# A four-layer graph network on one core: the last weights turned by VectorE, a new order between attention and mean, and a split chain of denominators

## The reference

```
L0 binary:    relu(adj @ (max(sign(x),0) @ sign(w).T))
L1 attention: h = x @ W_sa; s = s_left[:,None] + s_right[None,:]
              e = where(adj != 0, exp(-leaky_relu(s, 0.01)), 0)
              x_a = (e / (sum(e,1) + 1e-5)) @ h;   x_b = adj @ (x @ W_gcnb) + b
              sigmoid(attn_a * x_a + attn_b * x_b),  attn_* = sigmoid([adj @ x, x] @ W* + b*)
L2 mean:      (A @ (x @ W + b)) / deg,  A = (adj != 0), deg = column sums of A
L3 two GAT layers: Wh, Ws = split(x @ W_stack[l]);  a = softmax(Wh @ Ws.T) * adj
              x = leaky_relu(a @ Wh + x, 0.01)
```

## Time and profile before

| | |
|---|---|
| time, median of 3 runs | 476.89 us (476.69 to 477.68) |
| the profiled execution | 477.23 us, of which the span from first to last instruction is 475.4 |
| TensorE busy | 463.0 us, 97% of the span, 1854 instructions |
| VectorE busy | 372.1 us, 78% |
| ScalarE busy | 232.3 us, 49% |
| GpSimd busy | 190.6 us, 40% |
| DMA | 20.68 MB, 8180 packets, 44 GB/s on the mean |
| chain of work that ended last | TensorE 87%, VectorE 7%, issue 2%, DMA 2% |

### The profile page before, as it was taken

One profiled execution on the slowest core, in us unless ns is written; L12 is line 12 of the kernel. 1 busy time (PEld: TensorE's weight loads), 2 busy tenths in 40 slices (PEclk: granted clock), 3 DMA queues, 4 the chain that ended last, 5 costly groups with the idle time before them and its releaser, 6 DMA issues.

```text
span 475.4 us, 5636 instructions
## 1 busy us (share of the span) xinstructions
PE 463.0 (97%) x1854; PEld 304.2 (64%) x1854; DVE 372.1 (78%) x832; ACT 232.3 (49%) x411; POOL 190.6 (40%) x186
## 2 busy tenths in 40 slices
PE   8999999999999999999999999899999999999993
PEld 6999745545555588877544444454557546778882
DVE  4688799999998599739236757998755698799984
ACT  5979529980889653323334532251332475342200
POOL 1444665631425058823001541361430064456641
PEclk9999999999999999999999999999999999999999
DMA  8856310000364100000000000000000000000001
GB/s 280 284 181 193 123 40 0 1 1 0 117 193 161 32 0 1 0 1 1 1 0 0 0 1 1 1 0 1 0 1 0 1 1 1 0 13 22 23 22 40
DMA packets 8180, 20.68 MB, mean 44 GB/s; under 512 B 1008, under 2 KB 4740, under 8 KB 8152
## 3 DMA queue, kind: packets, MB, share of 16 engines
q1 hardware_dynamic: 7144, 19.02, 12.3%
q0 software_dynamic: 464, 0.79, 0.7%
q10 hardware_dynamic: 544, 0.52, 0.3%
HBM read 18.94 MB, written 1.39 MB: 43 GB/s over the span
## 4 chain that ended last, share of the span: by engine, by line
PE 87%; DVE 7%; issue 2%; DMA 2%; SPq 1%; ACT 1%; POOLq 0%; POOL 0%; DVEq 0%
PE psum L1544 19%; PE psum L1359 11%; PE psum L1335 11%; PE psum L1581 9%; PE psum L1644 8%; PE psum L1316 6%; PE psum L1422 6%; PE psum L1524 4%; PE psum L1237 2%; PE psum L1497 2%; PE psum L1379 2%; PE psum L1615 2%; PE psum L1406 2%; DMA adj_rows<-in_adj_dram 2%; PE psum L1476 1%
## 5 line engine op out<-in xcount | busy, mean ns | idle before, releaser
L1544 PE MATMUL psum<-QT,xT 128*128 128x512 f32 (+3 forms) x264 | 108.3, 542 | 1.7 <-ACT ST L634 1.7
L440 POOL TENSOR_TENSOR es<-es,ST 128x512 f32<-128x512 f32 (+3 forms) x60 | 74.9, 1248 | 53.8 <-ACT ST L639 52.1
L634 ACT ACTIVATE ST<-psum 128x512 f32<-128x512 f32 (+3 forms) x66 | 36.1, 546 | 89.6 <-DVE rm L994 77.9
L1544 PEld LDWEIGHTS psum<-QT,xT 128*128 128x128 f32 (+1 forms) x264 | 48.1, 186 | 44.5 <-issue 38.2
L994 DVE TENSOR_TENSOR rm<-psum,rm 128x512 f32<-128x512 f32 (+3 forms) x60 | 37.4, 624 | 41.2 <-PE psum L1544 41.0
L376 POOL TENSOR_TENSOR rstd<-veps,nhalf 128x1 f32<-128x1 f32 (+1 forms) x44 | 29.4, 668 | 65.0 <-DVE veps L770 65.0
L1644 PE MATMUL psum<-Wh,ST 128*128 128x256 f32 (+3 forms) x242 | 55.1, 380 | 0.0
L1581 PE MATMUL psum<-ST,Wh 128*128 128x512 f32 (+3 forms) x132 | 53.9, 542 | 0.0
L404 POOL TENSOR_TENSOR esumb<-esumb,eb 128x1354 f32<-128x1354 f32 (+1 forms) x10 | 34.5, 3447 | 46.4 <-ACT eb L528 46.4
L1359 PE MATMUL psum<-eb,x_all 128*128 128x512 f32 (+3 forms) x132 | 51.8, 542 | 0.0
L1335 PE MATMUL psum<-adjT,x_all 128*128 128x512 f32 (+3 forms) x132 | 50.1, 542 | 0.0
(11 more groups left out here) (181 smaller groups left out, 781.7 us busy)
## 6 DMA issues: line engine op xcount, KB each, us to landing
adj_rows<-in_adj_dram SPq DMA_DIRECT2D x10, 677.0 KB, 5.2
rows<-in_adj_dram SPq DMA_DIRECT2D x10, 677.0 KB, 4.0
x_all<-in_x_dram SPq DMA_DIRECT2D x5, 256.0 KB, 4.5
out_dram<-xs SPq DMA_DIRECT2D x10, 128.0 KB, 1.7
W<-in_L_gnn_W_stack_dram SPq DMA_DIRECT2D x2, 512.0 KB, 6.4
adj_rows<-in_adj_dram SPq DMA_DIRECT2D x1, 338.5 KB
rows<-in_adj_dram SPq DMA_DIRECT2D x1, 338.5 KB
w0n<-in_L_gnn_weight_dram SPq DMA_DIRECT2D x1, 256.0 KB, 2.8
```

Source lines behind the costliest of these rows:

```text
L440: nc.gpsimd.tensor_tensor(es[0:r, g % 2, 0:w], es[0:r, g % 2, 0:w], buf(g)[0:r, j, 0:w], ALU.add)\
L1544: last = nc.tensor.matmul(psum[0:r, SB[n % 3], 0:w], xT[l][:, k, j * P:j * P + r], QT[:, k, c0:c1], start=(k == 0), stop=(k == KD - 1))
```

## The change

SyncE loads W3 a second time, as 32x32 blocks laid out so that VectorE's block transpose yields the whole transpose. Each layer comes by four DMAs with runs of 32 elements, into space that exp buffers leave free, ahead of the loads of adjacency rows 9 and 10. VectorE turns each layer in one instruction, and TensorE's 16 transposes and ScalarE's four copies go. Each layer has its own W3T buffer and its own PSUM bank.

TensorE's first group of sum transposes moves one place up, into the last but one row of exp products, the second to its end, the third and the first projection in among the last row's products. ScalarE counts row 0 before its exp tile 6. VectorE reads the sums earlier, finishes `coef` with three instructions over full tiles (`dent` is set to 1 at the start), and scales tiles 3 to 10 and makes the degrees' reciprocals after the first sums of attention. The masks move, too. GpSimd's bias sums run at least four tiles late.

In the turnover from chunk 0 to 1, the denominators' chain goes in three parts behind rounds 1, 3 and 5, and scale, add and leaky go behind rounds 6, 7 and 8. All other turnovers stay as they are.

```diff
+            def load_blocks(l):
+                sp.wait_ge(h_step.sem, RING + l + 1)
+                sp.wait_ge(den_added.sem, RING + l + 1)
+                for a in range(QUADS):
+                    sp.dma_start(W3B[l][a * BLOCK:(a + 1) * BLOCK, :, :].rearrange("u e (b v) -> u e b v", v=BLOCK),
+                                 w3[l].rearrange("(b u) (e a v) -> a u e b v", u=BLOCK, a=QUADS, v=BLOCK)[a]).then_inc(w3b_in[l].sem, 16)
+
             sp.wait_ge(agga_done.sem, T)
             for i in range(T):
+                if i >= T - 2:
+                    load_blocks(i - T + 2)
                 if i >= 2:
                     sp.wait_ge(deg_ready.sem, T + i - 1)
...
             rsqrt(NB, 0)
-            for i in range(T):
+            rsqrt(NB, 1)
+            low_half(0)
+            low_half(1)
+            rsqrt(NB, 2)
+            low_half(2)
+            rsqrt(NB, 3)
+            for i in range(3, T):
                 if i + 1 < T:
                     rsqrt(NB, i + 1)
                 low_half(i)
+                if i >= 4:
+                    add_bias2(i - 4)
+            for i in range(T - 4, T):
                 add_bias2(i)
...
-            i = 0
             exp_scores(RING - 1)
+            row_degree(0)
+            i = 1
             for j in range(RING, T):
                 exp_scores(j)
-                for _ in range(2 if i + T - j < T else 1):
+                for _ in range(2):
                     if i < T:
                         row_degree(i)
                         i += 1
-            while i < T:
-                row_degree(i)
-                i += 1
...
-            w3T_evac(0)
             gate(0)
             gate(1)
             m3_evac(0)
+            m3_evac(1)
             gate(2)
-            w3T_evac(1)
             high_half(0)
             scale_b2(0)
-            m3_evac(1)
...
+            def turn_w3(l):
+                dve.wait_ge(w3b_in[l].sem, 16 * QUADS)
+                if l == 1:
+                    dve.wait_ge(h_step.sem, RING + 3)
+                    dve.wait_ge(den_added.sem, RING + 3)
+                nc.vector.transpose(W3T[l][:, :, :, :].rearrange("p h e n -> p (h e n)"), W3B[l][:, :, :].rearrange("p e n -> p (e n)"))\
+                    .then_inc(w3T_ready.sem, 1)
...
+            turn_w3(0)
             den_sums(0)
+            turn_w3(1)
+            den_sums(1)
             dve.wait_ge(att_t_ready.sem, 1)
             own.link(nc.vector.tensor_scalar(att[:, :, :], att_t[:, :, :], 0.5, 0.5, ALU.mult, ALU.add))
+            scale_xb(0, 3)
             den_sums(2)
+            dve.wait_ge(den_read.sem, BANKS_T)
+            own.link(nc.vector.tensor_scalar(dent[:, :], dent[:, :], ATTN_EPS, None, ALU.add))
+            own.link(nc.vector.reciprocal(dent[:, :], dent[:, :]))
+            nc.vector.tensor_tensor(coef[:, :], dent[:, :], att[:, :, 0], ALU.mult).then_inc(coef_ready.sem, 1)
...
+            attn_sum(0)
+            scale_xb(3, 6)
+            attn_out(0)
+            attn_sum(1)
+            scale_xb(6, T)
+            norm_apply(NB, 0, vbuf[:, 0, :])
+            attn_sum(2)
+            attn_out(1)
             dve.wait_ge(deg_ready.sem, 2 * T)
...
-            attn_sum(0)
-            attn_sum(1)
-            attn_out(0)
-            attn_sum(2)
+            norm_apply(NB, 1, vbuf[:, 1, :])
+            attn_sum(3)
             mean_mask(3)
-            for i in range(T):
+            attn_out(2)
+            attn_sum(4)
+            norm_apply(NB, 2, vbuf[:, 2, :])
+            mean_mask(4)
+            attn_out(3)
+            attn_sum(5)
+            mean_mask(5)
+            for i in range(3, T):
                 if i + 1 < T:
                     attn_out(i + 1)
                 norm_apply(NB, i, vbuf[0:kk(i), i % 4, :])
                 if i + 3 < T:
                     attn_sum(i + 3)
-                if i + 4 < T:
-                    mean_mask(i + 4)
+                if i + 3 < T:
+                    mean_mask(i + 3)
...
                 soft_step(g + 1, 0)
                 soft_step(g + 1, 1)
-                den_blocks(g)
+                if g > 0:
+                    den_turn(g)
+                    den_gather(g)
+                    den_spread(g)
                 for s in range(last):
                     both(g + 1, s)
-                    if s == 0:
+                    if g == 0 and s == 1:
+                        den_turn(g)
+                    if g == 0 and s == 3:
+                        den_gather(g)
+                    if g == 0 and s == 5:
+                        den_spread(g)
+                    if s == add - 1:
                         scale_t(g)
...
-            turnover(0, T, 2)
+            turnover(0, T, 7)
...
+                        if j == T - 2 and (c, m) == (1, 1):
+                            turn_exps(0)
+                        if j == T - 1:
+                            last.then_inc(h_done.sem, 1)
+                            if (c, m) == (1, 0):
+                                turn_exps(2)
+                            if (c, m) == (1, 1):
+                                h_proj(0)
...
                 if j == T - 1:
-                    turn_exps(0)
+                    turn_exps(1)
                 h_part(j)
...
-            h_proj(0)
-            turn_w3(0)
             h_proj(1)
             h_proj(2)
             mul_w3(0)
-            turn_w3(1)
+            mul_w3(1)
             h_proj(3)
-            mul_w3(1)
```

More of the change, by code:

```diff
@@ L556, in _ @@
                     nc.scalar.activation(hT[:, m, c0:c1], bank(c * KD + m, 0, c1 - c0), ACT.Copy).then_inc(hT_ready.sem, 1)
[L558 to L565 removed]
             def m3_evac(l):
                 act.wait_ge(m3_ps.sem, l + 1)
[L569 removed]
+                nc.scalar.activation(M3[:, l, :, :], bank(2 + l).rearrange("p (k n) -> p k n", k=KD),
                                      ACT.Copy).then_inc(m3_ready.sem, 1)
@@ L907, in den_sums, with scale_xb @@
                 last.then_inc(den_read.sem, 1)
+            def turn_w3(l):
[5 more added lines that the diff above has]
+                    .then_inc(w3T_ready.sem, 1)
+            def scale_xb(i0, i1):
+                for i in range(i0, i1):
+                    r = kk(i)
+                    last = nc.vector.tensor_scalar(xb[0:r, i, :], xb[0:r, i, :], att[0:r, i, 1:2], None, ALU.mult)
+                own.link(last)
@@ L1055, in den_blocks, with den_gather @@
                 own.link(nc.vector.tensor_reduce(quad[:, 0:nb], blocks[:, 0:nb * BLOCK].rearrange("p (b n) -> p b n", n=BLOCK), AX.X, ALU.add))
+            def den_gather(g):
+                nb = -(-chunk(g)[2] // BLOCK)
                 for a in range(QUADS):
@@ L1060, in den_blocks, with den_spread @@
                 own.link(nc.vector.reciprocal(quadsum[0:BLOCK, 0:nb], quadsum[0:BLOCK, 0:nb]))
+            def den_spread(g):
+                nb = -(-chunk(g)[2] // BLOCK)
                 for a in range(1, QUADS):
@@ L1350, in turn_exps, with h_proj @@
                 last.then_inc(den_ps.sem, 1)
+            def h_proj(i):
+                r = kk(i)
+                pe.wait_ge(hT_ready.sem, KD * ((i * P) // BANK + 1))
+                if i == 0:
+                    pe.wait_ge(wsa_in.sem, 16)
+                    pe.wait_ge(zp_read.sem, T)
+                if i == 1:
+                    pe.wait_ge(den_read.sem, BANKS_T)
+                if i >= 2:
+                    pe.wait_ge(gate_in.sem, i - 1)
+                for k in range(KD):
+                    last = nc.tensor.matmul(psum[0:r, 6 + i % 2, 0:D], hT[:, k, i * P:i * P + r], Wsa[:, k, :],
+                                            start=(k == 0), stop=(k == KD - 1))
+                last.then_inc(hp_done.sem, 1)
             def h_part(j):
@@ L1393, in _ @@
                         i += 1
-            def h_proj(i):
-                r = kk(i)
-                pe.wait_ge(hT_ready.sem, KD * ((i * P) // BANK + 1))
-                if i == 0:
-                    pe.wait_ge(wsa_in.sem, 16)
-                    pe.wait_ge(zp_read.sem, T)
-                if i == 1:
-                    pe.wait_ge(den_read.sem, BANKS_T)
-                if i >= 2:
-                    pe.wait_ge(gate_in.sem, i - 1)
-                for k in range(KD):
-                    last = nc.tensor.matmul(psum[0:r, 6 + i % 2, 0:D], hT[:, k, i * P:i * P + r], Wsa[:, k, :],
-                                            start=(k == 0), stop=(k == KD - 1))
-                last.then_inc(hp_done.sem, 1)
             def c_part(j):
```

70 lines of the change are left out of this document (20 added, 50 removed).

## The result

The changed kernel takes 475.34 us, median of 9 runs (473.92 to 475.69); the kernel before, in the same sessions, 477.58 us (9 runs, 476.69 to 478.68). The profiled execution of after took 473.92 us, span 472.1, against 477.23 and 475.4.

The account below looks back on a forecast made before the run. TensorE was taken to bound the kernel, with VectorE also full in the mean stage. Gains of 0.8 (mean stage) and 1.85 (chain) summed to 2.65 us: 477.23 to 474.6 profiled, median 474.2, range 472.7 to 476.3.

Parts of the forecast that it names:

- Bound: Whole kernel: TensorE busy 463.0 of 475.4 us, so savings count only where it does less or stops standing still.
- Part 1: Before the mean products: W3 transposes leave TensorE, 2.2 us less there; VectorE's two transposes, 1.24 us each, are free.
- Part 2: SyncE's block loads before the mean stage: 10 to 15 ns a piece, blocks there by 149 and 155, no cost.
- Price 0: SyncE's block loads and ScalarE's moved row count cost nothing unless the loads are late.
- Part 3: VectorE's order from attention to mean: tile 7 at about the same moment, TensorE waits eat 1.5 of 2.2 us.
- I take 0.8: Mean stage: the gain chosen in us, after the walk gave 206.5 against 207.2 for the stage's end.
- collisions: Mean stage, VectorE meeting GpSimd: late bias sums save 1.1 us, a new meeting with a scaling costs 0.2.
- walk: Four engines' queues followed from 154 us: mean products end at 206.5, waits of 0.7 and 0.8 before tiles 7 and 8.
- rival (b): Mean stage: collisions fall well and all 2.2 us come through, 472.8 us; chance 0.63 together with the forecast.
- the loss of 1.5 us: Mean stage: TensorE's waits before tiles 7 and 8, under the port lock; with a shared port the full 2.2 us.
- Part 4: Turnover from chunk 0 to 1: splitting the denominators' chain removes TensorE's stop, 1.85 us gained, bounds 1.2 to 1.9.
- (c): Before the mean stage: late block loads delay row 10, costing from a landing after 159.6, up to 488 us; chance 0.19.

Follow-up runs that it names:

- e3: The kernel before with only the W3 block loads and VectorE's two transposes added, none of the other edits: 481.66 us, ratio 1.0092.
- e7b: e3 with one more edit, ScalarE's first row count put ahead of the sixth round's exponentials: 476.37 us, ratio 0.9982 to the kernel before.
- e1: The changed kernel with chunk 0's denominators' chain whole again, ahead of the score tiles: 475.76 us, ratio 0.9958 to the kernel before.
- e6: The changed kernel with the two 128x512 instructions that begin chunk 0's chain put ahead of the score tiles: 473.48 us, ratio 0.9914 to the kernel before.
- e9: e8 with row 10's load issued ahead of the second block load: 477.24 us, ratio 1.0015 to the kernel before.
- e8: The changed kernel with both block loads one round (5.4 us) later: 478.57 us, ratio 1.0029 to the kernel before.

## Why the prediction was right, and where it was not

**Bound.** Right: what left TensorE and what stopped TensorE is the whole result (table).

**Part 1.** Right, and a little low. 2.2 us were to leave TensorE before the first mean product; from the start of the stretch that product came 2.56 us earlier (17.89 us, 171.89 - 154.00, instead of 20.45). 2.14 of it arrived: 0.1 went in the first group of mean products and 0.3 in the slow group of tile 3. VectorE's transposes took 1.23 us each (1.24 said). Neither held anyone up:

```profile
154.82 1.23 DVE L922 STREAM_TRANSPOSE W3T<-W3B 128x1024 f32<-128x1024 f32 x1
...
158.68 1.23 DVE L922 STREAM_TRANSPOSE W3T<-W3B 128x1024 f32<-128x1024 f32 x1
```

**Part 2.** Right in size: the pieces took 13 ns each on a DMA engine (8192 of them, 10 to 15 said, between bounds of 6 and 47), each of a layer's four DMAs landed 3.7 us after its issue at the median, the pieces of the two layers ended at 147.5 and 154.5 ("by 149 and 155"), row 10 landed at 156.87 ("near 156"), and the last count ended at 159.5 ("near 159"). The Trainium skill ("DMA: Bandwidth & Descriptors", section "Specifications") asks for 512 bytes; a piece of 128 bytes cost 2.2 times its share of a 1 KB packet's 47 ns, so the trace agrees that such pieces cost more than in proportion; of a read-modify-write no run shows anything. It was harmless here: each layer was there 4 us or more before its transpose started, and row 10 came 2.4 us before the landing from which it would have cost (157.2 on the clock of before, against 159.6). What was not seen is on what this reserve hangs: the one count on ScalarE that I had priced at nothing moves the start of the two block loads by 3.3 and 4.4 us (e3 against e7b). "Price 0" held for the whole change, but the load edit without the count costs 4.4 us more than the kernel before.

**Part 3.** The step that failed is the last: "I take 0.8". The terms before it were right or nearly so: first attention sum at 164.6 (164.34 in after), collisions -0.9 (-0.9), one mask fewer, idle +0.8 (+0.6; the prediction's 0.6 us of idle time before is 1.5 by busy time, and after has 2.1). Then a walk with an error of 0.6 us in the old order, and with 0.3 to 1.2 us between "late" and "in time", was used to price a stop. The right reading of its own remark (0.05 us longer delays give 0, no collision gives 2.3) would have been that the value lies anywhere from 0 to 2.2 with nearly even chances; it came out near rival (b), 2.14. The waits themselves were no phantom: the one before tile 8 came in three of seven profiled executions, at 0.4 us instead of 0.8. The Trainium skill's port lock ("SBUF — State Buffer", section "SBUF: two separate sides") agrees with the trace: 0.42 or 0.95 us where both engines work, as if one stood still for the other. But the loss of 1.5 us that I had hung on it didn't come: with the collisions that were left VectorE was in time by 0.85 us at tile 7 in after, and 0.4 us late at tile 8 in e1, e6 and e9.

**Part 4.** The mechanism was right (the stop of 1.71 us went, and the first twelve and the next four score products run as one), the sum was not. "VectorE never less than 1.2 us ahead" was wrong: the walk left out that GpSimd's additions stretch VectorE's instructions there, 3.8 us in all; and as VectorE stands for 1.71 us ahead of them, it had nothing to make this up with. Of 1.85 us came 1.33 in the turnover, and 0.46 was given back in the next, which the prediction didn't look at: 0.87, or 0.95 as timed by itself.

**Sum.** 0.8 + 1.85 = 2.65 stood against 2.14 + 0.87 = 3.0 in the traces and 2.6 by the ratio. One term was 1.3 too small and the other 1.0 too large; that the total fits is luck.

**Rivals.** (c) didn't happen, but e8 shows that it is real and that its threshold was right (2.95 us of stop for 3.1); its price was too low: a stop here can be paid twice, by the clock (5.98 us in the trace of e8).

## What to carry to other kernels

Price each moved instruction by what runs on GpSimd at its new place, compare the busy time of the engine that takes the work before and after, and look one stage further for what a now later engine gives back; then put a part of the moved work into an idle gap that is already there, as e6 does (0.9914 against 0.9945). An edit that hides nothing itself can carry the margin of another: follow each in-order queue back to what starts it, before calling a step free. When an engine-by-engine walk decides on a few tenths of a microsecond whether TensorE stops, give both outcomes their chance: here both were seen, in kernels with the same order.

## What the runs showed of the hardware

Where VectorE and GpSimd meet, either can be the one that waits. In the kernel before, VectorE's sum was stretched to 0.95 or 0.96 us for six tiles running, beside GpSimd's low halves. In after, with the same offset of 0.55 us between the two starts, VectorE took 0.42 us at 182.48 and 0.95 at 185.17. In both cases VectorE's mask product runs when GpSimd's low half begins, and the sum follows it; the first such mask of VectorE, and GpSimd's side of both:

```profile
181.71 0.86 DVE L883 TENSOR_SCALAR maskT<-adjT 128x1354 fp32r<-128x1354 f32 x1
```

```profile
181.93 1.57 POOL L421 TENSOR_TENSOR xhl<-x_all,xhl 128x256 fp32r<-128x256 f32 x1
...
184.62 1.22 POOL L421 TENSOR_TENSOR xhl<-x_all,xhl 128x256 fp32r<-128x256 f32 x1
```

The low half takes 0.73 alone. The lengths fit two engines that take turns: behind the mask (to about 182.6) first the sum, 0.42, then the low half, which ends at 183.50; or (mask to about 185.2) first the low half, which ends at 185.84, and then the sum, which ends at 186.12. Which goes first decides over 0.5 us on VectorE and 0.35 on GpSimd. What decides it was not found, and a walk can't know it. The second thing is the clock: a stop of 2.95 or 3.96 us at 165 us was followed by 6.0 and 6.5 us at 1.2 GHz in the profiled executions, which costs half of that, or nearly as much again as the stop; the stop of 1.71 us in the turnover of the kernel before and the 1.42 us in the profiled execution of e9 were followed by none.
